# Layer A's rows channel-major from the host, normed on GpSimd with moments spread by way of DRAM

## What is computed

```python
x = x + gnn(layernorm(x), adj, adj, ...)      # layer A: 12 heads of 32
x = x + ffn(layernorm(x), ...)                # layer B: 3 experts of width 128
# layernorm: (x - mean) / sqrt(var + 1e-5), over the 384 channels of a token
# gnn: q, k, v = h @ Wq.T, h @ Wk.T, h @ Wv.T + bv; softmax(q k' * 384**-0.5 + 2 adj) v; out @ Wo.T + bo
# ffn: gate = softmax(relu(h @ Wg1 + bg1) @ Wg2 + bg2), the best 2 of 3 experts;
#      per expert a causal attention over the 128 tokens (expert 0's q through a 3-tap convolution);
#      weighted by the gate, @ Wp + bp
```

## Time and profile before

| | |
|---|---|
| median of 3 runs (lowest to highest) | 2238.28 us (2237.51 to 2238.32) |
| the profiled execution: its time, its span | 2238.38 us, 2236.3 us |
| TensorE busy, matmuls | 2201.6 us (98%), 16941 |
| VectorE, ScalarE, GpSimd busy | 1903.9 us (85%), 1500.0 us (67%), 1157.3 us (52%) |
| TensorE clock granted, mean | 0.995 |
| DMA, mean | 64 GB/s |

### The profile page before, as it was taken

How to read it: one execution, slowest core, us unless ns; L and a number is a source line. 1 busy time by engine, 2 the same in 40 slices (tenths; PEclk the granted TensorE clock), 3 DMA queues, 4 the chain that set the end, 5 groups by cost and what they waited for, 6 DMA issues and landing times.

```text
span 2236.3 us, 51593 instructions
## 1 busy us (share of the span) xinstructions
PE 2201.6 (98%) x16941; PEld 1439.2 (64%) x16941; DVE 1903.9 (85%) x7152; ACT 1500.0 (67%) x5298; POOL 1157.3 (52%) x1551
## 2 busy tenths in 40 slices
PE   6999999999999999999999999999999999999998
PEld 4566666666666666666666666666666666666665
DVE  7888888888888888888888888888888888888895
ACT  5676766677666767666776667676667766667764
POOL 4645456454555454564545554555655445545452
PEclk8999999999999999999999999999999999999999
DMA  6222122221122221222221222211222212222110
GB/s 176 63 76 49 44 62 77 77 62 50 43 76 77 77 59 36 59 77 77 63 53 44 72 77 77 59 42 54 76 77 64 56 43 68 77 76 63 38 39 29
DMA packets 142265, 143.20 MB, mean 64 GB/s; under 512 B 16816, under 2 KB 141360, under 8 KB 142000
## 3 DMA queue, kind: packets, MB, share of 16 engines
q1 hardware_dynamic: 139808, 138.62, 23.3%
q10 hardware_dynamic: 2192, 1.29, 0.3%
HBM read 39.18 MB, written 25.17 MB: 29 GB/s over the span
## 4 chain that ended last, share of the span: by engine, by line
PE 94%; DVE 2%; SPq 1%; POOL 1%; issue 1%; DMA 0%; ACT 0%; DVEq 0%; POOLq 0%
PE B_bank L517 33%; PE A_bank L517 32%; PE A_bank L597 7%; PE A_bank L609 4%; PE B_bank L616 4%; PE A_bank L584 4%; PE B_bank L591 4%; PE B_bank L601 2%; PE A_bank L560 2%; PE B_bank L560 2%; SPq L492 1%; DVE raw_score L957 1%; DVE smax L963 0%; DMA Ks<-k_hi 0%; POOL S L1096 0%
## 5 line engine op out<-in xcount | busy, mean ns | idle before, releaser
L712 ACT ACTIVATE S<-raw_score,smin 128x128 f32<-128x128 f32 x1536 | 593.9, 393 | 172.9 <-DVE smin L957 172.9
L1096 POOL TENSOR_TENSOR S<-S,rowf 128x512 f32<-128x512 f32 x384 | 389.1, 1041 | 314.8 <-DVE rowf L982 314.8
L957 DVE CUSTOM_DVE_ANT_0 raw_score<-A_bank,adj,s_unit 128x128 f32<-128x128 f32 x1536 | 444.7, 346 | 4.3 <-PE A_bank L584 1.5
L1101 POOL TENSOR_TENSOR S<-S,row2f 128x384 f32<-128x384 f32 x128 | 106.0, 828 | 612.1 <-DVE row2f L990 611.9
L726 ACT ACTIVATE PT<-A_bank 128x512 f32<-128x512 f32 x384 | 220.1, 590 | 234.9 <-PE A_bank L597 234.9
L712 ACT ACTIVATION_READ_ACCUMULATOR S<-raw_score,smin 128x1 f32 x1536 | 296.0, 193 | 0.0
L597 PE MATMUL A_bank<-ident,S 128*128 128x128 f32 x1536 | 226.7, 274 | 3.6 <-DVE smin L957 2.5
L963 DVE TENSOR_REDUCE smax<-raw_score 128x12 f32<-128x1536 f32 x128 | 223.0, 1742 | 0.0
L597 PEld LDWEIGHTS A_bank<-ident,S 128*128 128x128 f32 x1536 | 187.0, 141 | 41.4 <-DVE smin L957 3.4
L719 ACT ACTIVATE S<-S,s2min 128x128 f32<-128x128 f32 x384 | 148.4, 390 | 3.0 <-DVE s2min L967 3.0
L584 PE MATMUL A_bank<-Ks,Qs 96*128 96x128 f16 x1536 | 140.6, 221 | 7.7 <-DMA Ks<-k_hi 5.0
(11 more groups left out here) (192 smaller groups left out, 6155.8 us busy)
## 6 DMA issues: line engine op xcount, KB each, us to landing
xin<-in_x SPq DMA_DIRECT2D x32, 768.0 KB, 4.5
Qs<-q_hi SPq DMA_DIRECT2D x256, 96.0 KB, 2.2
out<-x1res SPq DMA_DIRECT2D x128, 192.0 KB, 2.1
Ks<-k_hi SPq DMA_DIRECT2D x252, 96.0 KB, 2.3
Qs<-q_lo SPq DMA_DIRECT2D x128, 96.0 KB, 2.2
Ks<-k_lo SPq DMA_DIRECT2D x126, 96.0 KB, 2.3
adj<-in_adj SPq DMA_DIRECT2D x32, 256.0 KB, 3.4
S<-in_wq SPq DMA_DIRECT2D x1, 576.0 KB, 5.7
```

The lines of the kernel that those rows point to most:

```text
L712: ins = nc.scalar.activation(S[b % 2][:, h, :], raw_score[:, h, :], ACT.Exp, bias=smin[b % 2][:, h:h + 1], scale=-1.0, accum_out=ssum[b % ...
L957: ins = nc.vector.tensor_tensor_reduce(raw_score[:, h, :], src[:, j * T:(j + 1) * T], adj2[:, b, :], s_unit[:], 3.0e38, ALU.add, ALU.min, ...
L1096: nc.gpsimd.tensor_tensor(S[b % 2][:, hs, :], S[b % 2][:, hs, :], rowf[b % 2][:, hs].unsqueeze(2).broadcast_to([P, HPC, T]), ALU.mult).the ...
L1101: nc.gpsimd.tensor_tensor(S2[b % 2][:], S2[b % 2][:], row2f[b % 2][:].unsqueeze(2).broadcast_to([P, NE, T]), ALU.mult).then_inc(normed2, 1)
```

## The change

The host also hands over xT, the rows x of every group channel-major (128 channels, 3 chunks, 4 x 128 tokens). From group TURNED = 2 on, TensorE has no A.hT steps. Instead:

- SP loads xT of the group into xt (A.xT), a turn ahead.
- The moments are taken as before, from xin. SP stores -mean and 1/sqrt of the group's 512 tokens to DRAM (A.stat, in 4-byte pieces) and loads them back as two rows spread over all partitions, stat_wide (A.rows).
- GpSimd adds the one and multiplies by the other over all of xt (A.hx): two operations on 128x1536. Its four scalings into h1 go, except in groups 0 and 1.
- ScalarE's and VectorE's A.hT steps read xt in place of a bank of PSUM.

h1 now is a view of xt. All orders of steps are rewritten; of ORDER_OF_STEPS the new lines stand here, of the others nothing.

```diff
 ORDER_OF_STEPS = {
     "pe": """
-        A.score.0.0 A.score.0.1 A.v.0 A.v.1 A.score.0.2 B.hT.0 B.hT.1 B.hT.2 A.score.1.0 A.score.1.1 A.v.2
-        B.qk.0 B.v.0 B.v.1 A.score.1.2 B.qk.1 B.v.2 A.turn.0.0 A.v.3 A.turn.0.1 B.v.3 B.qk.2 A.turn.0.2 B.qk.3
-        A.hT.0 A.score.2.0 A.hT.1 A.mix.0 A.score.2.1 B.qk.4 A.hT.2 B.qk.5 A.turn.1.0 A.proj.0 B.score.0
-        A.turn.1.1 B.score.1 A.score.2.2 A.qk.0 A.turn.1.2 A.score.3.0 A.qk.1 A.qk.2 A.qk.3 B.turn.0 A.qk.4
-        B.mix.0 A.score.3.1 A.mix.1 A.score.3.2 B.turn.1 B.score.2 A.turn.2.0 A.qk.5 A.turn.2.1 A.proj.1
-        A.turn.2.2 B.score.3 B.mix.1 B.proj.0 A.mix.2 B.turn.2 B.proj.1 A.turn.3.0 B.mix.2 A.turn.3.1 A.turn.3.2
-        A.proj.2 B.turn.3 A.mix.3 B.mix.3 B.proj.2 A.proj.3 B.proj.3
+        A.score.0.0 A.v.0 A.score.0.1 A.score.0.2 B.hT.0 A.score.1.0 B.hT.1 B.hT.2 A.score.1.1 A.v.1 B.qk.0
+        B.qk.1 B.v.0 A.score.1.2 A.turn.0.0 A.score.2.0 B.qk.2 A.turn.0.1 A.score.2.1 B.v.1 B.v.2 A.turn.0.2
+        B.v.3 A.mix.0 A.turn.1.0 A.v.2 A.turn.1.1 B.qk.3 B.qk.4 A.score.2.2 A.turn.1.2 B.qk.5 A.proj.0 A.v.3
+        A.score.3.0 B.score.0 B.score.1 A.qk.0 A.qk.1 A.qk.2 A.score.3.1 A.qk.3 A.qk.4 B.turn.0 A.score.3.2
+        B.score.2 A.mix.1 B.turn.1 A.qk.5 B.mix.0 B.score.3 A.turn.2.0 A.turn.2.1 B.mix.1 A.turn.2.2 A.proj.1
+        B.turn.2 B.proj.0 A.mix.2 A.turn.3.0 A.turn.3.1 B.proj.1 A.turn.3.2 B.mix.2 B.turn.3 A.mix.3 A.proj.2
+        B.mix.3 A.proj.3 B.proj.2 B.proj.3
     """,
     "act": """
-        A.score.0.0 B.hT.0 B.hT.1 B.hT.2 A.score.0.1 A.score.0.2 B.qk.0 A.turn.0.0 B.qk.1 A.score.1.0 A.turn.0.1
-        A.score.1.1 A.turn.0.2 B.qk.2 A.hT.0 A.score.1.2 A.hT.1 B.gate.0 A.mix.0 B.qk.3 A.hT.2 B.qk.4 B.qk.5
-        A.turn.1.0 A.score.2.0 A.turn.1.1 A.score.2.1 A.qk.0 B.gate.1 B.score.0 A.qk.1 A.turn.1.2 A.score.2.2
-        B.score.1 A.qk.2 B.turn.0 A.qk.3 A.qk.4 A.score.3.0 B.mix.0 A.mix.1 B.turn.1 A.turn.2.0 A.score.3.1
-        B.score.2 A.score.3.2 A.turn.2.1 A.turn.2.2 B.mix.1 A.qk.5 A.mix.2 B.turn.2 B.score.3 A.turn.3.0 B.mix.2
-        A.turn.3.1 A.turn.3.2 B.turn.3 A.mix.3 B.mix.3
+        A.score.0.0 B.hT.0 B.hT.1 B.hT.2 A.score.0.1 A.score.0.2 B.qk.0 B.qk.1 A.score.1.0 A.score.1.1
+        A.turn.0.0 A.turn.0.1 B.qk.2 A.score.1.2 A.turn.0.2 A.turn.1.0 A.mix.0 B.qk.3 A.score.2.0 B.gate.0
+        A.score.2.1 B.qk.4 B.qk.5 A.turn.1.1 A.hT.0 A.hT.1 B.gate.1 A.hT.2 A.turn.1.2 A.score.2.2 A.qk.0 A.qk.1
+        B.score.0 A.score.3.0 A.qk.2 B.score.1 A.qk.3 A.qk.4 A.score.3.1 B.turn.0 B.score.2 A.mix.1 A.qk.5
+        B.turn.1 B.mix.0 A.score.3.2 A.turn.2.0 B.mix.1 A.turn.2.1 A.turn.2.2 B.score.3 A.mix.2 B.turn.2
+        A.turn.3.0 A.turn.3.1 A.turn.3.2 B.mix.2 B.turn.3 A.mix.3 B.mix.3
     """,
     "dve": """
-        A.score.0.0 A.v.0 A.score.0.1 A.score.0.2 B.hT.0 B.hT.1 B.hT.2 A.smax.0 A.v.1 A.score.1.0 B.v.0 A.norm.0
-        A.score.1.1 A.ln1 A.v.2 B.v.1 A.score.1.2 B.v.2 A.v.3 B.conv B.v.3 A.smax.1 B.gate.0 A.hT.0 A.norm.1
-        A.hT.1 A.score.2.0 A.mix.0 A.hT.2 A.score.2.1 B.gate.1 B.score.0 A.proj.0 A.score.2.2 B.score.1 B.gate.2
-        A.qk.0 B.norm.0 A.smax.2 A.qk.1 A.score.3.0 B.norm.1 A.norm.2 A.qk.2 A.qk.3 A.qk.4 A.score.3.1 A.mix.1
-        B.score.2 A.score.3.2 B.mix.0 A.smax.3 B.norm.2 A.norm.3 B.score.3 B.mix.1 A.qk.5 A.proj.1 B.proj.0
-        A.mix.2 B.norm.3 A.ln2.0 B.proj.1 A.ln2.1 B.mix.2 A.proj.2 A.mix.3 A.ln2.2 B.mix.3 B.proj.2 A.proj.3
-        A.ln2.3 B.proj.3
+        A.score.0.0 A.v.0 A.score.0.1 A.score.0.2 B.hT.0 B.hT.1 B.hT.2 A.smax.0 A.v.1 A.norm.0 A.score.1.0
+        A.score.1.1 A.ln1 A.score.1.2 B.v.0 A.smax.1 B.v.1 A.norm.1 A.score.2.0 A.score.2.1 B.conv B.v.2 B.v.3
+        A.mix.0 B.gate.0 A.score.2.2 A.v.2 B.gate.1 A.smax.2 A.hT.0 A.hT.1 A.hT.2 B.score.0 A.v.3 A.proj.0
+        A.score.3.0 B.gate.2 B.score.1 A.qk.0 A.qk.1 B.norm.0 A.qk.2 A.score.3.1 B.norm.1 A.score.3.2 B.score.2
+        A.norm.2 A.qk.3 A.qk.4 A.smax.3 A.mix.1 B.norm.2 B.score.3 B.mix.0 A.norm.3 A.qk.5 A.proj.1 B.mix.1
+        B.proj.0 A.mix.2 B.norm.3 A.ln2.0 B.proj.1 A.ln2.1 B.mix.2 A.mix.3 A.proj.2 A.ln2.2 B.mix.3 A.proj.3
+        B.proj.2 A.ln2.3 B.proj.3
     """,
     "pool": """
-        A.res.0 A.res.1 A.res.2 A.res.3 A.norm.0 A.ln1 B.res.0 B.res.1 B.res.2 B.res.3 A.norm.1 B.norm.0
-        B.norm.1 A.norm.2 B.norm.2 A.norm.3 B.norm.3 A.ln2.0 A.ln2.1 A.adj A.ln2.2 A.ln2.3
+        A.res.0 A.res.1 A.res.2 A.res.3 A.norm.0 B.res.0 A.ln1 A.norm.1 A.hx.0 B.res.1 B.norm.0 B.norm.1 B.res.2
+        A.norm.2 B.norm.2 B.res.3 A.norm.3 B.norm.3 A.adj A.ln2.0 A.ln2.1 A.ln2.2 A.ln2.3
     """,
     "sp": """
-        A.res A.stack.0 A.adj A.stack.1 B.proj.0 B.proj.1 B.proj.2 B.proj.3
+        A.res A.stat A.rows A.adj A.stack.0 A.stack.1 B.proj.0 B.proj.1 A.xT B.proj.2 B.proj.3
     """,
 }
```

```diff
@@ -477,6 +486,24 @@
                     if g == 0:
                         sp.wait_ge(h1_share_ready, 1)
                     sp.dma_start(xin[:], dram_group(x, following(g))).then_inc(x_loaded, 16)
+                if (stage, kind) == ("A", "xT") and not last:
+
+                    if following(g) == TURNED:
+                        wait_products(sp, ("A", "hT", KC - 1, 0), g)
+                    else:
+                        wait_evacuated(sp, ("A", "hT", KC - 1, 0), g)
+                    sp.dma_start(xt[:], xT[following(g)]).then_inc(xT_loaded, 16)
+                if (stage, kind) == ("A", "stat"):
+                    sp.wait_ge(rstd1_done, count(g, 1, 1))
+                    sp.dma_start(stat_rows[g].rearrange("q b t -> t q b"), stat[g % 2][:],
+                                 allow_slow_non_contiguous=True).then_inc(stat_stored, 16)
+                if (stage, kind) == ("A", "rows"):
+
+                    sp.wait_ge(stat_stored, count(g - TURNED, 16, 16))
+                    if g > TURNED:
+                        sp.wait_ge(hx_ready, count(g - TURNED, 1, 0))
+                    sp.dma_start(stat_wide[:], stat_rows[g].rearrange("q b t -> q (b t)").unsqueeze(0)
+                                 .broadcast_to([P, 2, GB * T])).then_inc(stat_spread, 16)
                 if (stage, kind) == ("A", "stack"):
...
                             act.dma_start(heads[n * HD:(n + 1) * HD, :, j, :],
                                           k_parts[n % 2][j * HD:(j + 1) * HD, :, :]).then_inc(ks_stacked, 16)
+                elif kind == "hT" and A and g >= TURNED:
+                    act.wait_ge(hx_ready, count(g - TURNED, 1, 1))
+                    if b == 0:
+                        wait_products(act, ("A", "v", GB - 1, 0), before(g))
+                        wait_products(act, ("A", "qk", 2 * KC - 1, 0), before(g))
+                    nc.scalar.activation(hT_hi["A"][:, b, :], xt[:, b, :], ACT.Copy, scale=H_SCALE)\
+                        .then_inc(hi_ready["ahead"], 1)
                 elif kind == "hT":
                     wait_products(act, step, g)
...
@@ -924,7 +958,8 @@
                 elif kind == "hT":
 
                     wait_hi(dve, step, g)
-                    nc.vector.scalar_tensor_tensor(out=hT_lo[stage][:, b, :], in0=src[:, :], scalar=H_SCALE,
+                    rows_T = xt[:, b, :] if turned(step, g) else src[:, :]
+                    nc.vector.scalar_tensor_tensor(out=hT_lo[stage][:, b, :], in0=rows_T, scalar=H_SCALE,
                                                    in1=hT_hi[stage][:, b, :], op0=ALU.mult, op1=ALU.subtract)\
                         .then_inc(freed, 1)
                 elif kind == "qk":
...
 
-            def layernorm1(g):
+            def statistics1(g):
                 pool.wait_ge(moments1, count(g, 1, 1))
-                nc.gpsimd.tensor_scalar(nmean1[:], mv1[:, :, 0], -1.0, None, ALU.mult)
+                if g >= TURNED + 2:
+                    pool.wait_ge(stat_stored, count(g - TURNED, 16, -16))
+                nmean1, rstd1 = stat[g % 2][:, 0, :], stat[g % 2][:, 1, :]
+                nc.gpsimd.tensor_scalar(nmean1, mv1[:, :, 0], -1.0, None, ALU.mult)
                 nc.gpsimd.tensor_scalar(ve1[:], mv1[:, :, 1], EPS, None, ALU.add).then_inc(vareps1, 1)
                 pool.wait_ge(vareps1, count(g, 1, 1))
-                nc.gpsimd.tensor_tensor(rstd1[:], ve1[:], half[:], ALU.pow).then_inc(rstd1_done, 1)
+                nc.gpsimd.tensor_tensor(rstd1, ve1[:], half[:], ALU.pow).then_inc(rstd1_done, 1)
+
+            def normed_rows1(g):
                 pool.wait_ge(rstd1_done, count(g, 1, 1))
                 for b in range(H1_POOL if g == 0 else GB):
-                    ins = nc.gpsimd.tensor_scalar(h1[:, b, :], xin[:, b, :], nmean1[:, b:b + 1], rstd1[:, b:b + 1],
-                                                  ALU.add, ALU.mult)
+                    ins = nc.gpsimd.tensor_scalar(h1[:, b, :], xin[:, b, :], stat[g % 2][:, 0, b:b + 1],
+                                                  stat[g % 2][:, 1, b:b + 1], ALU.add, ALU.mult)
                 ins.then_inc(h1_ready, 1)
 
             def split_lo(n):
...
-                    layernorm1(following(g))
```

(13 more changed lines are left out.)

146 lines of the change are left out of this document (78 added, 68 removed).

## The result

| | before | after |
|---|---|---|
| median (lowest to highest) | 2238.3 us (2237.5 to 2240.0) | 2410.9 us (2408.8 to 2415.4) |
| ratio, 95% interval | 1 | 1.0773 [1.0754, 1.0791] |
| span of the profiled execution | 2236.3 us | 2407.0 us |
| TensorE clock granted, mean | 0.995 | 0.964 |
| start of turns 1 and 2 (first matmul of A.score.0.0) | 44.0 and 89.0 us | 42.3 and 91.5 us |

What follows compares the result with a forecast made beforehand. TensorE's own stream of matmuls, busy all 68.17 us of a turn, was taken as the bound. A stand of 2.4 less 0.2 and 1.3 gave +0.9 us a turn, x30 = +28: 2266 us, range 2192 to 2325.

Steps and rivals of the forecast that it cites:

- the store: SP's store of the moments in 1024 pieces of 4 bytes: taken at 3 us, 2.1 below and 6 above.
- rival (c): Slow 4-byte store of 5.2 us, B.gate.0 released at 32 to 33: +2.6 us a turn, 2317 us; chance 0.15.
- The broadcast: SP's load of the moments spread over all partitions, 512 KB: taken at 3.9 us.
- The long operations: GpSimd's two operations over 128x1536: 3.4 us each, running from about 22.8 to 29.7 us of the turn.
- The hold: VectorE operations with both inputs in SBUF wait out GpSimd's long operation; TensorE stands 2.4 us a turn with hand-overs.
- A.turn.1.1's bank: Needed by A.score.3.0, freed 3.5 us after ScalarE's B.gate.0, at 33.8 to 34.7; TensorE there at 32.0.
- the end of B.gate.0: On VectorE, 0.5 to 1.4 us behind the second long operation, at 30.2 to 31.1 against 26.5 unheld.
- Rival (a): No hold that matters on VectorE, or one near 1 us: time falls by 39 us to 2199 us; chance 0.25.
- rival (b): GpSimd's long operations take 2.7 us each, TensorE stands about 0.8 us: -0.7 a turn, 2217 us; chance 0.15.
- What is removed: TensorE's three A.hT steps of four transposes, 0.44 us each: 1.3 us a turn, 39 us in all.
- small waits: TensorE's small waits of some 0.6 us a turn, of which 0.2 ahead of A.score.3.0 are swallowed by the stand.
- Start and end: Written-out parts around the turns: only orders rearranged and a first load added, 0 within 3 us either way.

Runs made afterwards that it cites:

- pieces32: The changed kernel with the moments stored in 128 runs of 32 bytes instead of 1024 of 4 (values land in another order): 2303.1 us.
- moments_turned_2: Changed kernel, moments transposed on TensorE and stored as 8 rows of 512 bytes, old first orders, VectorE's and ScalarE's steps moved around A.hT: 2241.5 us.
- moments_turned_0: Changed kernel's order of steps, moments transposed on TensorE and stored as 8 rows of 512 bytes, first orders of the kernel before: 2344.4 us.
- filler: The changed kernel with 40 transposes of the identity on TensorE ahead of A.qk.0, where TensorE stood: 2347.3 us.
- tiny_hx: pieces32 with GpSimd's two long operations on 12 columns instead of 1536, the other rows left unnormed: 2214.7 us.
- memset_hx: pieces32 with five GpSimd fills of all of xt in place of the two long operations, A's norm left out: 2213.3 us.
- token_major_first: token_major with evacuations ahead of the convolution, B.gate.0 behind A.hT.2, and the first group's orders of the kernel before: 2351.0 us.
- fast_moments: The changed kernel with 32-byte runs and right values, GpSimd reading the spread moments with a stride of 8 values: 2348.4 us.
- token_major: The changed kernel with 256 runs of 16 bytes, host's second copy token by batch, A.hT reading and writing every fourth element: 2350.4 us.
- orders_only: The new orders of steps with GpSimd's four scalings and TensorE's A.hT transposes back, no long operations: 2292.9 us against 2238.3 before.
- pieces32_split: pieces32 with GpSimd's two operations over 1536 columns cut into six over 512: 2279.9 us.

## Why the prediction was wrong

The direction was right, and the time (2266) was far off, beyond the range's upper end (2325).

**The step that failed: the store.** Its 1024 pieces were taken at 3 us, with 6 above. They take 9.5. The range's end for an unknown of this kind was no bound: 6 us was no row and no calculation, and rival (c) was worked out for 5.2 us only. Its last sentence has what happened: "Later still, ScalarE's and VectorE's A.hT wait for GpSimd itself, and A.qk.0 stands 3 us or more."

**The steps up to it.** The moments come at 15.5 us of the turn, predicted 15.7. The broadcast 4.2 us as the median and 5.6 in the turn shown, taken as 3.9. The long operations 3.43 to 3.44 us, taken as 3.4. The rows were to be spread at 22.8 and are at 30.7 in the turn shown (29.6 is the median): 6.5 of these 7.9 us are the store and 1.7 the broadcast. With a quick store the place was near: the operations start at 21.2 in pieces32 and at 22.4 in moments_turned_2.

**The hold.** Its mechanism was right: 3.3 to 3.8 us beside an operation of 3.4 to 3.9. So was its path, as pieces32 shows: ScalarE's B.gate.0 waits 4.34 us for VectorE, and 3.6 us behind it (forecast 3.5) A.turn.1.1's bank is free for A.score.3.0, at 35.3 us of the turn (forecast 33.8 to 34.7). Without the stands at B.qk.4 and A.v.3 TensorE would be there at 32.3 (forecast 32.0). So this bank by itself asks for 2.9 us, where the forecast had 2.4, and the two earlier stands lie within them, as the forecast said of A.v.3; that of B.qk.4 it did not have. Mis-sized was the end of B.gate.0: 0.5 to 1.4 us behind the second long operation, measured 2.7 (31.7 against 29.0), because g_hid waits for that operation's end as well and all of B.gate.0 follows. That 2.4 and 2.9 lie so near is in part luck: by the forecast's terms operations that end at 29.0 give a stand of 1.0 to 1.9. Rival (a) is refuted by L1057 and rival (b) by 3.44 us.

**The forecast with a quick store.** The store isn't all that was missing. The run nearest to the forecast's own case is moments_turned_0, with the changed kernel's order in the turn but for one transpose: long operations from 22.3 us (forecast 22.8), VectorE at B.gate.0 at 24.1 (forecast 24.1). It takes 2344 us, above the range too. B.gate.0's three products wait for the second operation instead of slipping in ahead of it, so it ends at 32.0 (forecast 30.2 to 31.1), and TensorE stands 2.75 us at A.v.3 with the lower clock behind it, 1.2 us more a turn.

**The place of the stand.** In the changed kernel it is A.qk.0, 4.4 us in the mean and 5.5 at most. A.score.3.0, the place of the forecast, has no stand there worth a row.

**The clock.** A second term that was put at nothing, without a word: no step had it, in the forecast or in (c), and it is 2.1 us a turn (filler). With a stand of 4.4 and 2.1 for the clock, less 1.3 and 0.2 by my own terms, rival (c) would have been +5 a turn, 2388 us.

**What is removed.** The three transposes were taken at 1.3 us a turn; measured are 68.17 - 67.18 = 1.0 (tiny_hx, memset_hx), and the 0.2 of small waits that I let the stand swallow didn't come on top. Where the remaining 0.3 went wasn't looked into.

**Start and end.** Put at 0 within 3 us: +2.5 up to the second turn in the changed kernel. In pieces32, tiny_hx, memset_hx and filler it is +5 to +7 (turn 2 begins at 94.2 to 95.6 against 89.0), though their first orders are the changed kernel's; the old first orders took 5.3 us back in token_major_first. With one and the same first orders the first turn is 49.2 to 49.5 us long in five kernels (the changed one, fast_moments, token_major, orders_only, pieces32_split) and 52.9 to 53.2 in the six others, against 45.0 before; what parts them stays open.

The sum as the runs give it, in us: removed work and the start -25 (2238 to 2213); hold +90 (to 2303); slow store +108 (to 2411), of which 64 come by the clock. These are the differences in the order in which the causes were taken away. They are not three parts of the changed kernel's turn: it has no stand at B.qk.4, A.v.3 or A.score.3.0, all its 4.4 us lie at A.qk.0, and no run has the slow store without the long operations. (The forecast's own last product, 0.9 x 30, is 27 and not 28; that changes nothing.)

## What to carry to other kernels

A transfer's price goes by its pieces: where a step cuts a small tensor into 4-byte elements, price it by piece, and where no row has such a piece, work the case out far beyond the longest transfer seen. A long GpSimd operation that reads SBUF is a hold of the same length on VectorE's SBUF-to-SBUF operations; it costs what is queued behind them, and an order that puts there only what nobody needs makes it free, as far as the engine has room (here it had none left for what was moved). A stand of TensorE of several microseconds should be priced with the slower matmuls behind it: 2.1 us behind stands of 4.4, and 1.2 or nothing behind stands of 2.75.

## What the runs showed of the hardware

- A store from 128 partitions to DRAM, 4 KB in all: 9.5 us (8.2 to 10.9) in 1024 pieces of 4 bytes, 2.2 in 256 of 16, 1.4 in 128 of 32. TensorE's transpose and a copy of 0.25 us make 8 rows of 512 bytes of it; these land within 1.2 us, where the broadcast's issue follows.
- GpSimd's addition over 128x1536: 3.44 us alone, 3.77 to 3.88 beside a held VectorE operation, 4.2 alone and 4.5 to 4.6 in the mean with the second input at a stride of 8 values. The hold costs GpSimd 0.3 to 0.4 us too.
- ScalarE's and VectorE's A.hT chunks (128x512): 0.62 and 0.68 us in order, 1.13 and 1.08 by every fourth element.
- GpSimd's fill doesn't hold a VectorE operation with two inputs in SBUF (767 ns), but it does hold g_hid, with one (1218 against 221).
- TensorE's clock: after a stand of 5.4 us 0.75 in the next 8.3 us; after one of 2.75 us 0.50 in the next 2.9 (moments_turned_0, the turn from 876.7), but 1.00 in three turns with the same stand. Behind the stands of 1.1 to 1.4 us in pieces32 it stayed at 1.00.
